# A two-layer graph transformer on one core: GpSimd's additions around norm2, a second turn written out by itself, and a value product in two halves

## The reference

```python
nx = _ln(x, ln1_g, ln1_b)
q = (nx @ wq + bq).reshape(b, s, H, HD).transpose(0, 2, 1, 3)      # k, v likewise
bias = jnp.where(adj_matrix > 0, 0.1 * edge_attr_matrix * adjf, -jnp.inf)[:, None]
attn = jax.nn.softmax(einsum('bhqd,bhkd->bhqk', q, k) / np.sqrt(HD) + bias, axis=-1)
x1 = residual + (out @ wo + bo)                 # out = attn @ v
n2 = _ln(x1, ln2_g, ln2_b)
x  = x1 + jax.nn.gelu(n2 @ w1 + b1, approximate=False) @ w2 + b2
# layer 1
w = jax.nn.softmax(where(adj == 0, -inf, Q @ K.T * scale), axis=-1)
y = x + (w @ V) @ Wo + bo
return layer_norm(y, gamma, beta)
```

## Time and profile before

| | us |
|---|---|
| median of 3 runs | 931.99 (927.68 to 933.8) |
| profiled execution | 936.33 |
| its span, from first to last instruction | 934.5 |
| TensorE busy | 872.8 (93%) |
| VectorE busy | 697.4 (75%) |
| ScalarE busy | 605.6 (65%) |
| GpSimd busy | 503.8 (54%) |

### The profile page before, as it was taken

One profiled execution on the slowest core, in us unless ns is written; L12 is line 12 of the kernel. 1 busy time (PEld: TensorE's weight loads), 2 busy tenths in 40 slices (PEclk: granted clock), 3 DMA queues, 4 the chain that ended last, 5 costly groups with the idle time before them and its releaser, 6 DMA issues.

```text
span 934.5 us, 22040 instructions
## 1 busy us (share of the span) xinstructions
PE 872.8 (93%) x7159; PEld 778.7 (83%) x7159; DVE 697.4 (75%) x2522; ACT 605.6 (65%) x1830; POOL 503.8 (54%) x374
## 2 busy tenths in 40 slices
PE   8998669999999999999999999999999999999896
PEld 8786459798888979888897988889798888989796
DVE  6686557878787877777787777778778787876646
ACT  5684746666767676676767667576766767584642
POOL 3532543746756464666646466664646656463512
PEclk9899779999999999999999999999999999999999
DMA  8100251523233252414324241432524143243001
GB/s 260 35 2 13 68 158 47 159 77 110 85 99 127 57 164 70 157 34 112 111 62 159 72 154 37 111 109 62 158 75 149 41 109 121 56 136 114 1 24 34
DMA packets 106304, 87.11 MB, mean 93 GB/s; under 512 B 3462, under 2 KB 91164, under 8 KB 106268
## 3 DMA queue, kind: packets, MB, share of 16 engines
q1 hardware_dynamic: 106252, 86.66, 30.8%
q10 hardware_dynamic: 16, 0.00, 0.0%
HBM read 47.85 MB, written 38.80 MB: 93 GB/s over the span
## 4 chain that ended last, share of the span: by engine, by line
PE 70%; DVE 7%; issue 5%; ACT 3%; DMA 1%; POOL 1%; DVEq 0%; SPq 0%; POOLq 0%
PE bank L401 20%; PE bank L403 19%; PE bank L402 19%; PE bank L562 3%; PE bank L718 3%; PE bank L586 3%; ACT p L1025 2%; DVE pT L1326 2%; DVE nx L1271 2%; PE bank L668 1%; DVE p L1398 1%; PE bank L497 1%; DMA p_s<-parked 1%; PE bank L711 1%; DVE mv L1261 1%
## 5 line engine op out<-in xcount | busy, mean ns | idle before, releaser
L961 ACT ACTIVATE p_s<-bank,neg_max 128x128 f32<-128x128 f32 x464 | 162.5, 389 | 90.8 <-DVE neg_max L1303 86.6
L1801 POOL TENSOR_TENSOR p_s<-p_s,rsum 128x512 f32<-128x512 f32 x116 | 118.1, 1041 | 189.6 <-DVE rsum L1310 189.6
L401 PE MATMUL bank<-w_hi,hT_hi 128*128 128x256 f32 x512 | 147.9, 289 | 1.3 <-DVE hT_lo L1195 1.3
L403 PE MATMUL bank<-w_hi,hT_lo 128*128 128x256 f32 x512 | 144.2, 282 | 0.0
L402 PE MATMUL bank<-w_lo,hT_hi 128*128 128x256 f32 x512 | 144.1, 282 | 0.0
L1303 DVE CUSTOM_DVE_ANT_0 bank<-bank,bias 128x128 f32<-128x128 f32 x464 | 117.5, 329 | 4.0 <-PE bank L562 3.8
L401 PE MATMUL bank<-n2T_hi,w_hi 128*128 128x512 f32 (+1 forms) x272 | 109.5, 403 | 7.6 <-DVE hT_lo L1195 7.6
L992 ACT ACTIVATE bank<-bank,vec_cols 128x512 f32<-128x512 f32 (+1 forms) x136 | 86.6, 637 | 34.0 <-PE bank L403 28.2
L961 ACT ACTIVATION_READ_ACCUMULATOR p_s<-bank,neg_max 128x1 f32 x464 | 106.4, 229 | 0.0
L402 PE MATMUL bank<-n2T_lo,w_hi 128*128 128x512 f32 (+1 forms) x272 | 104.6, 385 | 0.0
L403 PE MATMUL bank<-n2T_hi,w_lo 128*128 128x512 f32 (+1 forms) x272 | 104.6, 385 | 0.0
(11 more groups left out here) (233 smaller groups left out, 2494.8 us busy)
## 6 DMA issues: line engine op xcount, KB each, us to landing
parked<-pT SPq DMA_DIRECT2D x116, 256.0 KB, 4.0
pT<-parked SPq DMA_DIRECT2D x15, 1024.0 KB, 5.4
p_s<-parked SPq DMA_DIRECT2D x14, 1024.0 KB, 7.6
xs<-in_x SPq DMA_DIRECT2D x15, 512.0 KB, 3.8
out<-y SPq DMA_DIRECT2D x14, 512.0 KB, 2.9
adj_i<-in_adj SPq DMA_DIRECT2D x15, 256.0 KB, 2.7
out<-y SPq DMA_DIRECT2D x3, 256.0 KB, 2.2
x2T_f<-in_L_gnn_w SPq DMA_DIRECT2D x1, 512.0 KB, 6.8
```

The costliest lines, as they stand in the source:

```text
L401: mm(out, a_hi, b_hi, start=first, stop=False)
L403: return mm(out, a_lo, b_hi, start=False, stop=last)
L961: last = run(to, of, ACT.Exp, scale=-1.0, bias=neg_max[:, r, place:place + 1], accum_out=psum[:, r, place:place + 1])
L1801: P.tensor_tensor(p_s[:, r, :, :], p_s[:, r, :, :], rsum[:, r, :, None].to_broadcast([128, 4, NODES]), ALU.mult).then_inc(pool_p, 1)
```

## The change

In every turn with a full gp, GpSimd does `x2_plus_bo` ahead of the products of pair 1, asks rstd of norm2 behind three of these products, and does the fourth and `x_plus_bo` behind norm2. VectorE does the statistics of norm2 ahead of the third reciprocal, `moments` ahead of the block transposes and of the t copy, and spreads the transposes of pair 1 around `biased1` and `vo_copy`. TensorE does the first graph of `project_v(gp, 1)` ahead of the p transposes of layer 1 and the second behind them.

The turn for group 3 gets functions of its own on four engines. In it `scores(2, 1)` and all that hangs on it (`biased`, `exps`, `inverse`, `normal` and `blocks` of the second pair of group 2) stand behind the MLP's first half; they stood in the first turn. `mlp_down(1, ...)` stands in one piece ahead of the norm1 transposes of group 3. In the first turn layer 1 of group 0 comes ahead of most of the softmax of group 2, and GpSimd's additions ahead of its products.

```diff
             def project_v(g, q, graphs=(0, 1)):
...
+                for b in [2 * q + i for i in graphs]:
...
+                if graphs[-1] == 1:
+                    last.then_inc(pe_v, 1)
@@ TensorE, turn
                 n2_transpose(ga, True)
+                if size(gp) > 2:
+                    project_v(gp, 1, (0,))
                 p1_transpose(gb)
                 if size(gp) > 2:
-                    project_v(gp, 1)
+                    project_v(gp, 1, (1,))
@@ TensorE, first_turn
                 p1_transpose(0)
-                scores(2, 1)
                 project_v(2, 1)
                 attend1_pairs(0)
+
+            def second_turn():
+                for j in range(HT):
+                    mlp_up(1, j, True)
+                scores(2, 1)
+                mlp_down(1, 0)
+                mlp_down(1, 1)
+                norm_transpose(3)
+                project_k(3, 0)
+                project_k(3, 1)
+                x2_transpose(1)
+                project_q(3, 0)
+                project_q(3, 1)
+                t_project(1)
+                attend(2, 0)
+                attend(2, 1)
+                scores(3, 0)
+                out_project(2, 0)
+                out_project(2, 1)
+                project_v(3, 0)
+                scores1(1)
+                vo_project(1, 0, True)
+                vo_project(1, 1, True)
+                scores(3, 1)
+                n2_transpose(2, True)
+                p1_transpose(1)
+                project_v(3, 1)
...
@@ ScalarE, first_turn
                 t_copy(0)
+                exps1(0)
+                vo_copy(0)
                 exps(2, 0, 0)
-                exps(2, 0, 1)
-                exps1(0)
-                exps(2, 0, 2)
-                exps(2, 0, 3)
-                vo_copy(0)
                 n2T_copy(1)
                 p1T_copy(0)
...
+                exps(2, 0, 1)
+                exps(2, 0, 2)
                 v_copy(2, 1)
+                exps(2, 0, 3)
@@ ScalarE, second_turn
+                for j in range(HT):
+                    gelu(1, j)
+                run(probe[:, :], minus_half[:, 0:1], ACT.Exp)
+                for r in range(HPT):
+                    exps(2, 1, r)
+                nxT_copy(3)
...
+                vo_copy(1)
+                exps1(1)
+                exps(3, 1, 0)
+                n2T_copy(2)
+                p1T_copy(1)
+                exps(3, 1, 1)
+                v_copy(3, 1)
...
@@ VectorE, turn
                 residual1(ga, 1, True)
-                if whole:
-                    inverse(gp, 1, 2)
                 sums2(ga, 0)
                 sums2(ga, 1)
                 if whole:
-                    inverse(gp, 1, 3)
+                    inverse(gp, 1, 2)
+                moments(2, ga)
+                if whole:
                     blocks(gp, 1, 0)
                 t_copy(gb)
-                moments(2, ga)
+                if whole:
+                    inverse(gp, 1, 3)
+                norm2(ga)
                 if whole:
                     blocks(gp, 1, 1)
-                    blocks(gp, 1, 2)
-                norm2(ga)
                 biased1(gb)
                 if whole:
+                    blocks(gp, 1, 2)
+                vo_copy(gb)
+                if whole:
                     blocks(gp, 1, 3)
-                vo_copy(gb)
@@ VectorE, second_turn
+                for r in range(HPT):
+                    biased(2, 1, r)
+                residual2(1, 0)
...
+                attn_low(2, 0)
+                attn_low(2, 1)
+                for r in range(HPT):
+                    biased(3, 0, r)
+                inverse(3, 0, 0)
+                residual1(2, 0, True)
...
+                inverse(3, 0, 3)
+                blocks(3, 0, 1)
+                norm2(2)
+                biased1(1)
+                vo_copy(1)
...
+                residual3(1, 0)
+                residual3(1, 1)
+                for r in range(HPT):
+                    blocks(3, 1, r)
@@ GpSimd, first_turn and second_turn
                 x_plus_bo(2)
-                for r in range(HPT):
-                    normal(2, 0, r)
-                for r in range(HPT):
-                    normal(2, 1, r)
                 x1_plus_b2(1)
                 mask1(1)
                 move_up(2)
+                for r in range(HPT):
+                    normal(2, 0, r)
+
+            def second_turn():
+                rstd(1, 3)
...
@@ GpSimd, turn
-                for q in pairs(gp):
-                    for r in range(HPT):
-                        normal(gp, q, r)
-                x_plus_bo(gp)
+                for r in range(HPT):
+                    normal(gp, 0, r)
+                x2_plus_bo(gb)
+                if size(gp) > 2:
+                    for r in range(3):
+                        normal(gp, 1, r)
                 rstd(2, ga)
                 pool.wait_ge(ln_dve[2], ln_end(ga))
-                x2_plus_bo(gb)
+                if size(gp) > 2:
+                    normal(gp, 1, 3)
+                x_plus_bo(gp)
                 x1_plus_b2(ga)
```

More of the change, by code:

```diff
@@ L803, in first_turn @@
                 p1_transpose(0)
-                scores(2, 1)
                 project_v(2, 1)
                 attend1_pairs(0)
+            def second_turn():
[24 more added lines that the diff above has]
+                project_v(3, 1)
+                pe.wait_ge(act_vo, 2)
+                attend1(1, 0)
+                pe.wait_ge(dve_vo, 1)
+                pe.wait_ge(act_v, pair0(3) + 2)
+                attend1(1, 1)
             def last_turn(ga, gb):
@@ L882, in _ @@
             first_turn()
-            turn(3, 2, 1)
+            second_turn()
             with pe.Fori(3, GROUPS - 2) as g:
@@ L1476, in turn @@
                     h_low(gb, j)
-                if isinstance(ga, int) and ga == 2:
-                    for r in range(HPT):
-                        blocks(ga, 1, r)
                 sums3(gc)
@@ L1571, in first_turn, with second_turn @@
                 biased(2, 0, 0)
+                biased1(0)
                 norm2(1)
[L1573 to L1576, removed]
                 inverse_sums1(0)
+                for r in range(1, HPT):
+                    biased(2, 0, r)
                 n2T_low(1)
+                residual3(0, 0)
                 for r in range(HPT):
                     inverse(2, 0, r)
-                biased(2, 1, 0)
-                biased(2, 1, 1)
+            def second_turn():
+                sums1(3)
+                moments(1, 3)
@@ L1583, in first_turn @@
                 blocks(2, 0, 0)
                 blocks(2, 0, 1)
-                biased(2, 1, 2)
-                biased(2, 1, 3)
-                residual3(0, 0)
+                h_low(1, 0)
+                norm1(3)
+                h_low(1, 1)
                 blocks(2, 0, 2)
                 blocks(2, 0, 3)
+                h_low(1, 2)
+                sums3(0)
+                h_low(1, 3)
+                moments(3, 0)
+                h_low(1, 4)
+                h_low(1, 5)
+                norm3(0)
@@ L1590, in first_turn @@
+                h_low(1, 6)
+                h_low(1, 7)
+                for r in range(HPT):
+                    biased(2, 1, r)
+                residual2(1, 0)
                 for r in range(HPT):
                     inverse(2, 1, r)
+                    if r:
+                        blocks(2, 1, r - 1)
+                blocks(2, 1, 3)
+                residual2(1, 1)
+                nxT_low(3)
+                x2T_low(1)
+                t_copy(1)
+                attn_low(2, 0)
+                attn_low(2, 1)
@@ new lines, in second_turn @@
+                for r in range(HPT):
+                    biased(3, 0, r)
+                inverse(3, 0, 0)
+                residual1(2, 0, True)
+                inverse(3, 0, 1)
+                blocks(3, 0, 0)
+                residual1(2, 1, True)
+                sums2(2, 0)
+                sums2(2, 1)
+                inverse(3, 0, 2)
+                moments(2, 2)
+                inverse(3, 0, 3)
[3 more added lines that the diff above has]
+                vo_copy(1)
@@ L1593, in last_turn @@
+                blocks(3, 0, 2)
+                blocks(3, 0, 3)
+                for r in range(HPT):
+                    biased(3, 1, r)
+                n2T_low(2)
+                inverse_sums1(1)
+                for r in range(HPT):
+                    inverse(3, 1, r)
+                residual3(1, 0)
+                residual3(1, 1)
+                for r in range(HPT):
+                    blocks(3, 1, r)
             def last_turn(ga, gb, gc):
@@ L1689, in _ @@
             first_turn()
-            turn(3, 2, 1, 0)
+            second_turn()
             with dve.Fori(3, GROUPS - 2) as g:
@@ L1820, in first_turn, with second_turn @@
                 move_up(2)
+                for r in range(HPT):
+                    normal(2, 0, r)
+            def second_turn():
+                rstd(1, 3)
+                pool.wait_ge(ln_dve[1], ln_end(3))
```

(19 more changed lines are left out.)

26 lines of the change are left out of this document (19 added, 7 removed).

## The result

| | before | after |
|---|---|---|
| median of four runs, us | 930.66 (927.68 to 933.8) | 896.95 (896.26 to 897.17) |
| profiled execution, us | 936.33 | 897.06 |
| its span, us | 934.5 | 895.2 |
| mean granted clock | 0.965 | 0.991 |

The ratio is 0.9636, with an interval of 0.9601 to 0.9671: 33.7 us faster. The forecast was 914 and its range 898 to 926, so the change gained more than the range allowed, by 1 us.

A forecast was written before the change was run, and what follows sets the result against it. TensorE was bound by its wait for biased1 at the norm2 transposes, behind GpSimd's addition, and secondly by the clock. 932.0 - 10.8 (loop turn) - 5.5 (low clock) - 2 (second turn) = 913.7, forecast 914; 905 to 922, overall range 898 to 926.

The forecast's parts named there:

- the wait named: TensorE ahead of the norm2 transposes, waiting for biased1: 24.8 us in 15 waits of up to 1.8, said to go.
- the variance's hold: VectorE's norm2 variance, held until GpSimd's addition ends: 1.64 us against 0.17 elsewhere; after the change, held by a product.
- the low pieces of the loop: Loop stretches at 1.2 GHz, 1.45 us each: three quarters were to go, 5.5 of 7.3 us in the median run.
- Gain per turn: 0.9 us: Loop turn, shorter by the earlier norm2 chain less new waits: bounds 0.5 to 1.77, 10.8 us over twelve turns.
- the three small waits: New TensorE waits in the loop turn: 0.5 at scores1, 0.23 at the value product, 0.3 at attend1.
- Taken: 2 us faster: Second turn, with group 4's norm1 transposes at 176.6 instead of 182.73, less 4.4 for low clock; bounds 8 faster, 5 slower.
- the eight waits laid out: TensorE, second turn and the one after: h_low 3, nxT 1.7, parked blocks 1.9, residual1 2.6, biased1 1.9, p1T 2.3, v 1.1, 4.3.
- three low pieces: Second turn: three or so stretches at 1.2 GHz, 1.45 us each, taking back 4.4 of the 6.1 us gained.
- The value split: Value product of pair 1 in two halves around the p transposes, filling the time exps1 runs: costed at nothing.
- The cover of the x load: Loop turn: next x lands at 227.0, statistics want it at 227.6; 0.6 us left where there were over 5.
- rival (c): Loop turn: x load lands in 7.6 us instead of 3.8, TensorE loses 2.8 per turn: 953, chance 0.05.
- Rival (a): Small waits don't arise, second turn keeps its full gain: 19 for the loop, clock 7, second turn 6: 900, chance 0.20.

The follow-up runs named there:

- filled: Kernel before with 14 products of the identity put ahead of the norm2 transposes in each turn: 938.79 us, ratio 1.0104.
- at 0.30: Kernel before with the changed order on GpSimd only, TensorE and VectorE in their old loop order: 912.78 us, ratio 0.9852.
- at 4.2: Changed kernel with GpSimd's loop turn as before, TensorE and VectorE keeping the new order: 972.67 us, ratio 1.0473 to the kernel before.
- the kernel with the addition one place later: Changed kernel with x_plus_bo behind x1_plus_b2 on GpSimd in the loop turn: 918.59 us, ratio 0.9899 to the kernel before.
- the kernel with the second turn alone: Changed kernel with the old loop turn on TensorE, VectorE and GpSimd, so only first and second turn changed: 925.06 us, ratio 0.9936.

## Why the prediction was wrong in size

The direction and the mechanism were right: the wait named is gone, with most of the variance's hold (0.66 against 1.64) and the low pieces of the loop. Against the median of 932.0 that the sum started from, its terms were 10.8 for the loop turn, 5.5 for the low pieces and 2 for the second turn. Measured are 18.2 (12 x 1.52) for the loop turn, 5.7 by the traces or 7.3 by the medians for the second turn, and the rest, 9.5 to 11, which must be low-clock pieces in the loop and the start, though no run measured it by itself: 35.0 instead of 18.3.

- **"Gain per turn: 0.9 us" is the first term that was mis-sized: 1.52.** The chain up to norm2 was right in its order and in what holds it. The variance is held until the product ends, 258.77 against 258.75, for 0.66 us where 0.7 was laid out; the Trainium skill's rule (SBUF — State Buffer, section "Who interferes with whom", whoever issues first has the shared ports for the whole instruction) says the same, and the trace agrees. What failed are the three small waits charged behind it: 0.5 at scores1, 0.23 at the value product, 0.3 at attend1. Measured are 0.08 (scores1 starts that much later against residual1 than in the earlier trace rows), none that is marked, and 0.07. The layout put each step behind the full length of the one ahead, but on VectorE the rows overlap by about 0.1 (residual1 ends at 256.24, the statistics start at 256.15). So by the t copy it was 0.43 late, by norm2 0.63, by the vo copy's end 0.34, and the p transposes took 0.60 instead of 0.90. Errors of a few tenths in one direction were written down as waits.
- **"Taken: 2 us faster" is the second: 5.7 to 7.3.** The length laid out held. From the norm2 transposes of the first turn to the norm1 transposes of group 4 it took off 6.1 (182.73 less 176.6), and 6.8 came: 92.26 in before (from 90.47), 85.48 in after (from 88.24). In part that is luck: the eight waits laid out sum to 18.8 and those in after to 13.4, and two pieces at 1.2 GHz (1.7 and 1.9 us) took up most of the difference. One by one it is 1.51 + 0.64 for h_low where 3 stood, 1.57 for 1.7, 2.19 for 1.9, 2.05 for 2.6, 2.45 for 2.3, and 3.03 for 4.3 in the turn after. Those for biased1 (1.9) and v (1.1) are not in the profile of after, where a piece at 1.2 GHz stands in front of them; in other kernels with the same second turn they are 1.65 to 1.71 (four kernels) and 0.35 to 0.78 (three). What failed is the 4.4 charged on top for three low pieces, since the profile of before has such pieces in its own 182.73. Stretches of before, columns as in the earlier trace rows:

```profile
91.00:101.00 10.00, 5.82 (x51) 4.98 (x50) 5.90 (x42) 6.79 (x32) 3.45 (x4) 0.69 0.17 55
112.00:122.00 10.00, 6.27 (x15) 4.49 (x16) 6.69 (x13) 4.07 (x7) 7.77 (x7) 0.50 0.00 0
131.00:142.50 11.50, 6.13 (x102) 5.03 (x102) 2.10 (x7) 2.03 (x4) 0.09 (x1) 0.70 0.64 223
```

  In after the clock is 1.00 from 91 to 142.5, and there are two pieces behind that (from 144.6 and from 158.3, each behind a wait), the first of which only takes the time of the wait for biased1:

```profile
142.50:173.00 30.50, 24.04 (x149) 20.02 (x150) 24.38 (x98) 20.67 (x75) 18.46 (x16) 0.89 0.33 87
```

  So the low clock was a gain of the change here and was booked as a cost.
- **The low pieces in the loop** went altogether, not by three quarters. The reason given, that the piece belongs to the long wait, holds: filled, the wait brings none; at 0.30 none; at 1.77 it brings some; at 4.2 a longer one in every turn. That the piece stands right behind the wait no row of the prediction shows, but the trace does: in the turn of before from 383.29 the granted clock is 0.50 from 385 to 388, from 1.7 behind the wait's end.
- **The value split** was costed at nothing, and is worth nothing.
- **The cover of the x load** was given as 0.6 and is 0.3 to 0.4: the load is issued 0.6 earlier than laid out and the statistics start 0.7 earlier, and the load lands in 4.3 instead of 3.8. The slower rival (c) named the right place; the kernel with the addition one place later shows its price: issued 2.4 later (0.41 ahead of layer 1's division, at 271.62, against 2.77 in after, at 267.95), 1.8 per turn. It did not come because the landing grew by 0.5 and not by 3.8.
- **Rival (a)**, 900, had it nearly right, with a second turn of 6. The range ended at 898, since it took the loop term to 16, short of that term's own bound of 21 and of the 18.2 that came, and did not add the upper ends of all three terms.

## What to carry to other kernels

A slow engine's long instruction can stand in the critical chain though its engine is half idle; ask what the waiting step has queued ahead of it on each engine, and move the orders of both sides together, since one side alone gave half the gain here and the other alone made the kernel slower. In a layout by hand, sum the steps with their overlaps, and don't charge a wait that is smaller than the error of the steps in front of it. When a stretch is compared with its own time before, look first at what the clock was in that time before a low clock is added to the new one.

## What was not expected of the hardware

- A single wait of 1.77 us in a turn brought a piece at 1.2 GHz in eight turns of the profiled execution of before and in five of the kernel with the second turn alone, with the same wait in the turns that had none. In both the turns with a piece follow each other without a gap. Runs of one kernel spread by 13 us with it (before: 922.1 us at a mean granted clock of 0.981 to 934.9 at 0.966); why the pieces begin and end at those turns stays open.
- Two longer waits show it at once: the norm2 transposes behind 3.90 us of idle took 1.94 instead of 1.09, and attend1 behind 2.45 took 3.83 instead of 1.97. But in after 2.05 brought a piece only 1.3 later (144.6), and 2.19 (136.08) none.
- The 14 identity products took 3.29 us, some 0.23 each and 28 instructions in the trace, which is why filling the wait cost more than the wait.
- The 512 KB load lands in 4.2 to 4.3 us in the eight kernels where the stores of the blocks follow it at once on the queue, and in 3.8 in the four where they don't; no run moved the stores alone.
